# Routed token rows gathered in quarters and turned by VectorE instead of TensorE, with a reordered chunk 0 and reordered up programs

## The reference, cut to what matters

```
xn = layernorm(x)                                   # [8, 1024, 512]
proj = xn @ W1 + b1                                 # 512 -> 3 x 1024: hidden, forget, input
h_t = sigmoid-like gates of proj, scanned over t    # log_g, softplus, cumlogsumexp in the reference
s  = h @ W2 + b2                                    # 1024 -> 512

logits = xn @ gate_w                                # 512 -> 32
e = argmax(logits); score = sigmoid(max(logits))
xs = xn * score, sorted by expert
routed = (silu(xs @ routed_gate_w[e]) * (xs @ routed_up_w[e])) @ routed_down_w[e]
shared = (silu(xn @ shared_gate_w) * (xn @ shared_up_w)) @ shared_down_w
out = x + s * silu(shared + routed)
```

## Time and profile before

| | |
|---|---|
| median of 3 runs | 3959.93 us (3959.68 to 3960.81) |
| the profiled execution | 3965.17 us |
| its span (first to last instruction in the records) | 3963.4 us |
| mean granted TensorE clock | 0.991 |
| TensorE, VectorE, ScalarE, GpSimd busy | 97%, 52%, 50%, 20% of the span |
| shared sweep, recurrence, routed stage | 0 to 1160, 1160 to 2599, 2608 to 3947 us |
| HBM read and written | 364.73 and 102.99 MB, 118 GB/s over the span |

### The profile page before, as it was taken

One profiled execution on the slowest core, in us unless ns is written; L12 is line 12 of the kernel. 1 busy time (PEld: TensorE's weight loads), 2 busy tenths in 40 slices (PEclk: granted clock), 3 DMA queues, 4 the chain that ended last, 5 costly groups with the idle time before them and its releaser, 6 DMA issues.

```text
span 3963.4 us, 57336 instructions
## 1 busy us (share of the span) xinstructions
PE 3853.3 (97%) x19580; PEld 3291.8 (83%) x19583; DVE 2080.7 (52%) x3042; ACT 1980.6 (50%) x2668; POOL 780.4 (20%) x840
## 2 busy tenths in 40 slices
PE   7999999999989999999999999989999999999998
PEld 6888888888867788888888888878999998998987
DVE  5232332323246755555555555566666767677674
ACT  3222222222227667676776767754445545455453
POOL 2011010110105100000000000023334344343433
PEclk9999999999989999999999999999999999999999
DMA  4212121121211110000001000066666767677673
GB/s 157 78 75 85 53 93 66 77 82 58 80 53 44 47 69 32 32 32 32 32 32 64 32 32 32 21 218 229 208 233 229 263 217 265 236 266 248 222 264 122
DMA packets 273545, 466.43 MB, mean 118 GB/s; under 512 B 25402, under 2 KB 172987, under 8 KB 269636
## 3 DMA queue, kind: packets, MB, share of 16 engines
q1 hardware_dynamic: 235860, 346.48, 25.5%
q0 software_dynamic: 37616, 119.08, 8.7%
HBM read 364.73 MB, written 102.99 MB: 118 GB/s over the span
## 4 chain that ended last, share of the span: by engine, by line
PE 54%; issue 6%; ACT 4%; DVE 4%; DVEq 1%; DMA 1%; ACTq 0%; POOL 0%; another core or an unknown queue 0%; POOLq 0%; SPq 0%
PE bank L87 12%; PE bank L89 12%; PE bank L88 12%; PE bank L1716 9%; PE bank L1106 5%; PE bank L1110 3%; ACT whi L1367 2%; DVE th L1601 1%; PE bank L1666 1%; ACT thT L1513 1%; DVEq L1249 1%; DVE hs L986 1%; DMA harmless<-in_L_attn_x,at_x 0%; ACT L953 0%; ACT tsg L1504 0%
## 5 line engine op out<-in xcount | busy, mean ns | idle before, releaser
L87 PE MATMUL bank<-txT,whi 128*128 128x256 f32 (+2 forms) x2048 | 616.4, 301 | 23.7 <-issue 13.1
L88 PE MATMUL bank<-txT,whi 128*128 128x256 f32 (+2 forms) x2048 | 610.6, 298 | 0.0
L89 PE MATMUL bank<-txT,wlo 128*128 128x256 f32 (+2 forms) x2048 | 610.5, 298 | 0.0
L87 PE MATMUL bank<-xT,w_hi 128*128 128x512 f32 x1536 | 598.9, 390 | 1.8 <-DVE b2all L1011 1.8
L88 PE MATMUL bank<-xT,w_hi 128*128 128x512 f32 x1536 | 598.7, 390 | 0.0
L89 PE MATMUL bank<-xT,w_lo 128*128 128x512 f32 x1536 | 598.5, 390 | 0.0
L1371 DVE TENSOR_TENSOR wlo<-raw,whi 128x2048 fp32r<-128x2048 f32 x186 | 425.9, 2290 | 116.2 <-ACT whi L1367 97.5
L549 DVE TENSOR_TENSOR h_act<-h_act,psU 128x512 f32<-128x512 f32 x128 | 88.0, 688 | 687.6 <-PE psU L89 685.2
L87 PEld LDWEIGHTS bank<-txT,whi 128*128 128x128 f32 x2048 | 391.7, 191 | 30.7 <-issue 14.4
L1716 PE MATMUL bank<-whi,thT 128*128 128x512 f32 x1264 | 410.9, 395 | 4.2 <-issue 4.2
L88 PEld LDWEIGHTS bank<-txT,whi 128*128 128x128 f32 x2048 | 392.0, 191 | 1.2
(11 more groups left out here) (207 smaller groups left out, 7699.5 us busy)
## 6 DMA issues: line engine op xcount, KB each, us to landing
raw<-in_L_ffn_routed_gate_w SPq DMA_DIRECT2D x124, 512.0 KB, 3.7
raw<-in_L_ffn_routed_up_w SPq DMA_DIRECT2D x124, 512.0 KB, 5.1
raw<-in_L_ffn_routed_down_w SPq DMA_DIRECT2D x124, 512.0 KB
xT_dram<-xT SPq DMA_DIRECT2D x16, 2048.0 KB, 6.3
xT<-xT_dram SPq DMA_DIRECT2D x14, 2048.0 KB, 7.9
xs_dram<-x_in SPq DMA_DIRECT2D x16, 1024.0 KB, 4.4
ss_dram<-y_sb SPq DMA_DIRECT2D x64, 256.0 KB, 2.0
ss_dram<-ry SPq DMA_DIRECT2D x64, 256.0 KB, 2.6
```

The costliest lines, as they stand in the source:

```text
L87: pe.matmul(out, w[0], x[0], start=start, stop=False)
L88: pe.matmul(out, w[0], x[1], start=False, stop=False)
L89: return pe.matmul(out, w[1], x[0], start=False, stop=stop)
```

## The change

**Token rows.** A piece's rows are gathered as quarter rows: `xs_dram` is seen as 4 x 8192 rows of 128 values, and a group of 128 tokens takes four gathers, each of 128 quarter rows (512 B), in place of one of 128 rows of 2 KB. In gather j, partition 32b + i takes quarter b of token 32j + i. VectorE turns the group's tile with one STREAM_TRANSPOSE in 32 by 32 blocks (`turn_x` moves from TensorE to VectorE), into a new tile `xt`. After it partition 32b + r holds value 128b + 32k + r of every token, so the weight rows are loaded in the order that fits: each gate or up part is loaded by four transfers of 32 partitions each in place of one, eight for a part in place of two. `x_hi` and `x_lo` read the tile in SBUF in place of a PSUM bank, and all three groups are turned and split at the end of the piece's up part. The four PSUM transposes per group, and the first piece's twelve, go.

**Row numbers.** The gather numbers are four times the row plus the quarter of the partition (`quarter`, a column set once by GpSimd). The table is read back in two layouts and transposed twice. For the gathers of `ss` and `xr`, GpSimd copies the scatter numbers and limits them in a second step in each piece.

**Places.** Several tiles move by 2 KB, and the load of part 2 of expert 1 waits for the outputs of the recurrence as well.

**Chunk 0.** SP's stores and the load of chunk 2's tokens come behind all weight parts; ScalarE's scores come in block 2 in place of 3; VectorE's four statistics of chunk 2 come together behind the last block.

**Up programs.** `by_size` asks `n < sizes[half]` with the smaller sizes in the first branch.

```diff
-        elif key == (1, TILES - 1):
-            store_xT(0, 0, 0)
-            store_xs(0, 0, 0)
-            if NCH > 2:
-                load(2, 0, 1)
+    store_xT(0, 0, 0)
+    store_xs(0, 0, 0)
+    if NCH > 2:
+        load(2, 0, 1)
...
-            if b == 3 and isinstance(c, int) and c == 0:
+            if b == 2 and isinstance(c, int) and c == 0:
...
-            if more2 and b >= NI - TILES:
+            if more2 and b >= NI - TILES and not (isinstance(c, int) and c == 0):
                 stats_of(*nxt2(c, j, it), b - NI + TILES)
         h_lo(c, NI - 1)
+        if more2 and isinstance(c, int) and c == 0:
+            for q in range(TILES):
+                stats_of(*nxt2(c, j, it), q)
...
+    xs_quarters = xs_dram.rearrange("t (b n) -> (t b) n", b=STEP)
...
-    at_x = k.sb("at_x", [P, WIDE], I32)
+    at_x = k.sb("at_x", [P, GROUPS * STEP], I32)
...
     half = len(sizes) // 2
-    with eng.If(n > sizes[half - 1]):
+    with eng.If(n < sizes[half]):
+        by_size(eng, n, body, sizes[:half])
+    with eng.Else():
         by_size(eng, n, body, sizes[half:])
-    with eng.Else():
-        by_size(eng, n, body, sizes[:half])
...
-        return [w[e].rearrange("(k p) i -> p k i", p=P)[:, :, q * 2 * P:(q + 1) * 2 * P] for w in (rgw, ruw)]
+        return [w[e].rearrange("(b k r) i -> b r k i", b=STEP, r=UNIT)[:, :, :, q * 2 * P:(q + 1) * 2 * P]
+                for w in (rgw, ruw)]
...
     for m, w in enumerate(part(q, e)):
-        dst = pair(raw_of(q, e))[:, m] if q < D0 else raw_of(q, e)[:, 2 * m:2 * m + 2, :]
-        sp.dma_start(dst, w).then_inc(raw_loaded[q], 16)
+        if q < D0:
+            for b in range(STEP):
+                sp.dma_start(pair(raw_of(q, e))[b * UNIT:(b + 1) * UNIT, m], w[b]).then_inc(raw_loaded[q], 16)
+        else:
+            sp.dma_start(raw_of(q, e)[:, 2 * m:2 * m + 2, :], w).then_inc(raw_loaded[q], 16)
...
         for b in range(STEP):
             runs = tok_dram[b * UNIT:(b + NU) * UNIT].rearrange("(j i r) a -> i j (r a)", i=UNIT, r=UNIT)
             sp.dma_start(places[b * UNIT:(b + 1) * UNIT], runs).then_inc(places_loaded, 16)
+            rows = tok_dram[0:NU * UNIT].rearrange("(j i r) a -> i j (r a)", i=UNIT, r=UNIT)
+            sp.dma_start(unit_rows[b * UNIT:(b + 1) * UNIT], rows).then_inc(places_loaded, 16)
...
         if q == RING - 1:
             sp.wait_ge(*freed["split"])
             sp.wait_ge(*freed["state"])
+            sp.wait_ge(*freed["outputs"])
...
-    act.wait_ge(raw_loaded[q], (e + 1) * 32)
+    act.wait_ge(raw_loaded[q], (e + 1) * 16 * (2 * STEP if q < D0 else 2))
...
+    def fetch_x():
+        for g in range(GROUPS):
+            for j in range(STEP):
+                fetch(xg[g][:, j, :], xs_quarters, at_x[:, g * STEP + j:g * STEP + j + 1], xg_loaded[g])
     def first_tokens(pool):
-        pool.wait_ge(table, 4)
-        pool.tensor_copy(at_x[:], gather_at[:, 0:WIDE]).then_inc(at_x_done, 1)
+        pool.wait_ge(table, 6)
+        pool.tensor_copy(at_x[:], gather_at[:, 0:GROUPS * STEP]).then_inc(at_x_done, 1)
         pool.wait_ge(at_x_done, 1)
+        fetch_x()
+        pool.tensor_scalar(at_s[:], scatter_at[:, 0:WIDE], T - 1, None, ALU.min).then_inc(at_s_done, 1)
+        pool.wait_ge(at_s_done, 1)
         for g in range(GROUPS):
-            fetch(xg[g][:], xs_dram, index(at_x, g), xg_loaded[g])
-        for g in range(GROUPS):
-            fetch(harmless[:], x_rows, index(at_x, g), out_stored[g])
+            fetch(harmless[:], x_rows, index(at_s, g), out_stored[g])
             pool.wait_ge(out_stored[g], 16)
 
...
+    for b in range(STEP):
+        pool.memset(quarter[b * UNIT:(b + 1) * UNIT], float(b)).then_inc(quarter_set, 1)
+        pool.wait_ge(quarter_set, b + 1)
...
-            pool.wait_ge(xg_loaded[g], (p + 1) * 16)
+            pool.wait_ge(xg_loaded[g], (p + 1) * 16 * STEP)
...
-        pool.tensor_copy(at_x[:], gather_at[:, bass.ds(nxt, WIDE)]).then_inc(at_x_done, 1)
+        pool.tensor_copy(at_x[:], gather_at[:, bass.ds(nxt, GROUPS * STEP)]).then_inc(at_x_done, 1)
...
         pool.wait_ge(turned_x, (p + 1) * GROUPS)
         settle(pool, settled)
-        for g in range(GROUPS):
-            fetch(xg[g][:], xs_dram, index(at_x, g), xg_loaded[g])
+        fetch_x()
...
-        pool.tensor_copy(at_s[:], gather_at[:, bass.ds(u, WIDE)]).then_inc(at_s_done, 1)
-        pool.wait_ge(at_s_done, p + 1)
+        pool.tensor_copy(at_s[:], scatter_at[:, bass.ds(u, WIDE)]).then_inc(at_s_done, 1)
+        pool.wait_ge(at_s_done, p * 2 + 2)
+        settle(pool, settled)
+        pool.tensor_scalar(at_s[:], at_s[:], T - 1, None, ALU.min).then_inc(at_s_done, 1)
+        pool.wait_ge(at_s_done, p * 2 + 3)
...
+def by_unit(a, g):
+    return xT[:, a, :, g * P:(g + 1) * P].rearrange("p k (j i) -> p j k i", i=UNIT)
...
-        act.activation(xT[:, 0, :, turned(g)], bank_x(p, g), ACT.Copy).then_inc(xhi, 1)
+        act.activation(by_unit(0, g), xt[g][:], ACT.Copy).then_inc(xhi, 1)
...
-            if b == NI - 1:
-                act.wait_ge(u_mm, p * NI + NI)
-                x_hi(p + 1, 0)
...
-        if first:
-            hi(1)
-            x_hi(p + 1, 1)
-            hi(2)
-            x_hi(p + 1, 2)
-            hi(NQ - 1)
-        else:
-            hi(NQ - 1)
-            for g in range(1, GROUPS):
-                x_hi(p + 1, g)
+        act.wait_ge(u_mm, p * NI + NI)
+        for g in range(GROUPS):
+            x_hi(p + 1, g)
+        for q in range(1 if first else NQ - 1, NQ):
+            hi(q)
...
-        dve.tensor_tensor(xT[:, 1, :, turned(g)], bank_x(p, g), xT[:, 0, :, turned(g)], ALU.subtract)\
-            .then_inc(xlo, 1)
+        dve.tensor_tensor(by_unit(1, g), xt[g][:], by_unit(0, g), ALU.subtract).then_inc(xlo, 1)
...
-        dve.wait_ge(places_loaded, 16 * STEP)
+        dve.wait_ge(places_loaded, 16 * 2 * STEP)
         dve.transpose(scatter_at[:, 0:NU], places[:].rearrange("p j r -> p (j r)")).then_inc(table, 1)
+        dve.transpose(gather_at[:, 0:NU], unit_rows[:].rearrange("p j r -> p (j r)")).then_inc(table, 1)
         dve.memset(gather_at[:, NU:NU + 16], 0).then_inc(table, 1)
         dve.memset(scatter_at[:, NU:NU + 16], T).then_inc(table, 1)
-        dve.wait_ge(table, 3)
-        dve.tensor_scalar(gather_at[:, 0:NU], scatter_at[:, 0:NU], T - 1, None, ALU.min).then_inc(table, 1)
+        dve.wait_ge(table, 4)
+        dve.tensor_scalar(gather_at[:, 0:NU], gather_at[:, 0:NU], T - 1, STEP, ALU.min, ALU.mult)\
+            .then_inc(table, 1)
+        dve.wait_ge(table, 5)
+        dve.wait_ge(quarter_set, STEP)
+        settle(dve, settled)
+        dve.tensor_scalar(gather_at[:, 0:NU], gather_at[:, 0:NU], quarter[:, 0:1], None, ALU.add)\
+            .then_inc(table, 1)
...
+    def turn_x(p, g):
+        dve.wait_ge(xg_loaded[g], (p + 1) * 16 * STEP)
+        at_least(dve, xlo, p * GROUPS)
+        dve.transpose(xt[g][:].rearrange("p j k i -> p (j k i)"), xg[g][:].rearrange("p j n -> p (j n)"))\
+            .then_inc(turned_x, 1)
...
         dve.sem_inc(h_done, 1)
+        for g in range(GROUPS):
+            turn_x(0, g)
...
-            if b == NI - 1:
-                x_lo(p + 1, 0)
...
+        for g in range(GROUPS):
+            turn_x(p + 1, g)
         lo(0 if first else 2)
-        x_lo(p + 1, 1)
-        lo(1 if first else NQ - 1)
-        x_lo(p + 1, 2)
-        if first:
-            lo(2)
-            lo(NQ - 1)
+        for g in range(GROUPS):
+            x_lo(p + 1, g)
+        for q in range(1 if first else NQ - 1, NQ):
+            lo(q)
...
-    def turn_x(p, g):
-        pe.wait_ge(xg_loaded[g], (p + 1) * 16)
-        at_least(pe, xlo, p * GROUPS + g)
-        for kb in range(KD):
-            mm = pe.transpose(psX[:, kb, :], xg[g][:, kb * P:(kb + 1) * P], ident[:])
-        mm.then_inc(turned_x, 1)
-    def passed_x(p, g):
-        pe.wait_ge(xlo, p * GROUPS + g)
-        pe.sem_inc(turned_x, 1)
...
-    def first_turns(pe):
-        for g in range(GROUPS):
-            pe.wait_ge(xg_loaded[g], 16)
-            pe.wait_ge(*freed[("bank 0", "bank 2", "bank 3")[g]])
-            for kb in range(KD):
-                mm = pe.transpose(first_turned(g)[:, kb, :], xg[g][:, kb * P:(kb + 1) * P], ident[:])
-            mm.then_inc(turned_x, 1)
...
-    pe.wait_ge(*freed["bank 1"])
+    for n in range(1, 4):
+        pe.wait_ge(*freed[f"bank {n}"])
...
-            if b == NI - 2:
-                turn_x(p + 1, 0)
...
-            turn_x(p + 1, 1)
...
-            ahead = pe.value_load(listed[0:1, 1, bass.ds(p + 1, 1)], min_val=LEAST, max_val=MOST_UNITS)
-            third(pe, ahead, lambda: turn_x(p + 1, 2), lambda: passed_x(p + 1, 2))
```

More of the change, by code:

```diff
@@ L1088, in vector, with tensor @@
         output(NCH - 1)
-    def tensor(pe, before_last):
+    def tensor(pe):
         pe.wait_ge(small, 16)
@@ L1194, in recurrent_and_routed @@
         xT = place("txT", [P, 2, KD, PIECE], 96, F32R)
-        raw = [place(f"raw{n}", [P, 4, 512], at) for n, at in enumerate((108, 116, 134))]
```

(24 more changed lines are left out.)

14 lines of the change are left out of this document (4 added, 10 removed).

## The result

The changed kernel takes 4131.41 us (median of 4 runs, 4129.27 to 4147.10) against 3960.37 us: a ratio of 1.0438 (95% interval 1.0424 to 1.0453), 171 us slower. The forecast was 4055, its range ended at 4110. The sign and the engine were right, the size was not.

The account below looks back on a forecast made before the run. TensorE, busy 97%, was taken to bound the kernel, with GpSimd's list becoming the routed stage's period after the change. +96 + 16 - 10 - 8 = +94 gave 4055 us, own range 4000 to 4105, 8-in-10 range 3957 to 4110.

Parts of the forecast that it names:

- part 2: Routed stage: GpSimd's list, with nine more gathers per piece, becomes the period, 43.7 us for 256-column pieces; +96 us.
- Rival B: Routed stage: GpSimd's wait swallows the added issues, TensorE gets its transposes back in full; 3911 us, chance 0.09.
- Rival C: Weight ring: each part lands 2 us or more too late for its L1367; +60 us, 4115 us, chance 0.10.
- Rival A: Routed stage: the added gather issues are not stretched, the cycle is 38.7 us; 3955 us in total, chance 0.13.
- rival D: Branch still costs 6 us, chunk-0 wait moves to its end; +18 us, 4073 us, chance within the forecast's 0.68.
- part 4: Weight loads: eight transfers of 32 partitions for a gate/up part instead of two, costed at 0.
- part 3: Routed stage: three turns per piece add 2.1 us on VectorE, which has the room (819 of 1201 us busy).
- part 1: Routed stage: TensorE loses its transposes, saving at most 40.6 us of the 1200.9.
- Chunk 0: -10 forecast: Chunk 0: the wait for chunk 2's tokens goes, and the low clock with it; -10 us, between -5 and -10.5.
- The recurrence: +16 forecast: Recurrence: nine more first gathers and the index step fall through to TensorE, with low clock behind; +16 us.
- the lower bound's reason: Recurrence: GpSimd's waits for the harmless gathers shrink by as much, leaving +3 us.
- Entering the stage: -8 forecast: Routed stage's entry: the 256-column program is fallen into, 6 us gone and 2 of low clock; -8 us.

Follow-up runs that it names:

- experiment 1: Kernel before with only the gathers changed, twelve of 512 B per piece in place of three of 2 KB: 4109.65 us, ratio 1.0374.
- experiment 8: Changed kernel with each gate or up part loaded by two transfers of 128 partitions as before, twelve gathers kept: 4105.84 us, ratio 1.0362.
- experiment 7: Changed kernel with VectorE's L1377 on a quarter of its columns from the second expert on, twelve gathers kept: 3961.09 us, ratio 0.9998.
- Experiment 6: Changed kernel with GpSimd's wait for the gathers' landing moved from a piece's end to ahead of the next at_s copy: 4086.15 us, ratio 1.0318.
- experiment 9: Kernel before with gate and up parts loaded by eight transfers of 32 partitions in place of two, nothing else: 3973.73 us, ratio 1.0029.
- Experiment 3: Changed kernel with three gathers of whole rows per piece and two transfers for each weight part: 3950.48 us, ratio 0.9972.
- experiment 12: Kernel before with the change's chunk 0 and its up programs by size: 3949.23 us, ratio 0.9964.
- experiment 5: Changed kernel with three gathers of whole rows, VectorE's turns left out from the second piece on, landing waits kept: 3928.36 us, ratio 0.9915.
- experiment 2: Changed kernel with three gathers of whole rows per piece in place of twelve: 3959.09 us, ratio 0.9992.

## Why the prediction was wrong in size

**Right: GpSimd's list becomes the period (part 2's mechanism).** The wait ahead of the scatter went, VectorE's sum waits for `yo_free`, and twelve gathers alone cost 148 us. VectorE's order is felt as forecast as well: its turns waited 75.3 us in the stage for gathers to land, and TensorE 41.3 us for the low parts behind them. Rival B falls with experiment 1. Rival C falls with experiment 8, and with the trace of the changed kernel, in whose 29 pieces no weight part came too late for its split. Rival A, the cycle of 38.7, is about what experiment 7 shows when VectorE is out of the way; the trace of the changed kernel has 47.2. Of rival D, chunk 0's wait did move to its end in part (3.3 us of TensorE's time), and the slow branch moved behind the first piece's up part.

**Wrong: "Together 26.8 us ... With the added issues 26.8 + 11.5 + 0.45 = 38.7", and 43.7 with the stretching.** The stretching was sized well: over the 29 pieces the gathers take 714.6 us here and 533.1 in experiment 7, 6.3 per piece, of which the kernel before had some 2, so 4.3 were added; the forecast added 5. What is missing from the sum is time that is not an issue: the landing of the last gathers. The list was counted from GpSimd's instructions, and the wait `landed` at its end was put at nothing, as it was always met in the earlier trace rows, where the gathers are issued 14 us before the scatter. Once the slack is eaten, a landing of 10 us sits right behind the last issue. It enters at two places.

Behind the last scatter GpSimd waits for it: in the piece shown 2.6 us, and 2.0 for a copy that thereby falls under an L1377. That is 4.6 where 47.2 against 43.7 is 3.5, because the gathers came out cheaper: from the first of the twelve to the copy of the scatter indices it is 30.4 us (3143.43 to 3173.80), 14.3 before (3100.92 to 3115.26), 16.0 more where the forecast had 11.5 + 0.45 + 5 = 16.95.

In pieces with three groups VectorE's third sum waits for it, which delays the third scatter: 32.4 us of waits in the stage.

From first scatter to first scatter in GpSimd's timeline, the cycle of the pieces with two groups is 47.1 us on average where 43.7 stood in the forecast, that of the pieces with three 48.4 where 45.3 stood. In the first, the idle time ahead of the copy of at_x and the copy itself took 3.3 us more than before; in the second, the idle time ahead of the third scatter 2.5 more. Some 3 us in each of 29 pieces are about the 83 us by which the stage's 1380.1 exceeds the forecast's 1296.7. Experiment 6 takes the first place away and gets 45 us back; the cycle with two groups is then 43.4 us.

**Wrong: "I cost it 0" (part 4, the weights).** 11.6 us alone, 25.6 in the changed kernel. Two things were seen. In experiment 9 ScalarE's splits waited for their weights 14 times in the stage, 13.3 us in all, nearly always for a down part, and never in the kernel before: rival C's wait, at a small part of its size. In the changed kernel no split in the stage waited so, but with two transfers the gathers landed 2 us earlier (experiment 8). On the rule cited there from the Trainium skill ("DMA: Bandwidth & Descriptors"), that 32 partitions keep all 16 engines, these runs say only that 32-partition transfers cost more DMA time for the same bytes: a share of 0.84 in experiment 9 against 0.69.

**Wrong, but hidden: "VectorE has the room" (part 3) and the 40.6 us of part 1.** The turns stand in a stretch where VectorE has no gap. Experiment 3 against experiment 12 (-11.7 and -12.9 us, the first is the second with the turns moved and the new row numbers) puts what moving the turns nets at about +1 us, which is no difference by their intervals: the gain of part 1 is all given back, 31 us of it by experiment 5. So rival A's sum, -5 us, has a hole too. That experiment 7 comes near it (-1 us) does not bear it out, for there VectorE's list is shortened as well; with that list at full length 256-column pieces last 38 to 40 us even where GpSimd has room (experiment 2).

**The Trainium skill's inference** ("SBUF — State Buffer", Who interferes with whom), that a tensor_tensor with two SBUF inputs leaves descriptor generation alone, does not hold for these indirect gathers: in experiment 7 gathers of 1848 ns became 1051 when such an instruction was shortened. It was right to weigh it as the less likely. What exactly the two engines meet at no run here shows; an indirect gather also reads its row numbers from SBUF.

**The small parts.** Chunk 0: -10 forecast, -9.2 measured alone. The recurrence: +16 forecast, +10.6 in the trace; the lower bound's reason held in part, as the wait for a harmless gather shrank by 6.0. Entering the stage: -8 forecast, -3.6 measured; the step "fallen into: 6 us gone" failed, since the jump over the other programs comes some 28 us later.

**Slips in the working.** "The difference is GpSimd's wait of 13.56" is misread: 36.55 less 26.8 is 9.75, and the 13.56 hold the 3.8 of VectorE's sums too. The stretches 2 + 0.5 + 1.5 + 1.5 are 5.5, not 5, and two 384-column pieces of 49.75 instead of 45.3 add 8.9, not 7. Put right, the sum would be about 4069, which changes no conclusion.

**What stays open.** In the stage the parts alone add to 132.5 (gathers) + 6.3 (eight transfers) - 1.1 (turns, experiment 3), 138 of 179 us. Experiment 8's 35.5 us in the stage, against 6.3 alone, cover 29 of the other 41. The last 12 were not taken apart; the profiled execution's own 11 us may be among them. How much of all this the lower clock of 0.93 adds wasn't separated either.

## What to carry to other kernels

When an engine with slack becomes the loop, count its whole list, with the waits that were always met: a wait for a transfer's landing costs nothing until the list has no slack left to hide it. An engine's average share says little about the stretch where the work is put; read the timeline there for gaps before calling added work free. And an edit that takes work from the bounding engine is worth only the distance to the next list, here VectorE's 21.9 us against TensorE's 18.5 or so.

## What the runs showed of the hardware

A gather of 128 rows of 512 B took GpSimd as long as one of 2 KB (1254 and 1174 ns in the stage, 1005 with VectorE out of the way), so four of them cost four times as much. It is not only gathers that last longer beside VectorE: a copy of 128x12 numbers on GpSimd took 2.23 us beside a VectorE instruction with two SBUF inputs, 0.19 otherwise. Only two or three of TensorE's branches between the up programs are slow in each run, all within the routed stage's first pieces: 6.27, 5.24 and 4.20 us before, 6.37 and 4.79 after, 3.29 and 6.19 in experiment 12. Reordering the programs moves the first from the entry to behind the first up part; that they are slow because the code had not run yet is a guess.
